# Experts' tokens placed in DRAM buckets in four groups, and the first expert steps put among the last attention tiles

## The reference

```python
x = x + L0_xattn(layernorm(x), ctx)        # 16 heads of 16
x = x + L0_ffn(layernorm(x))               # experts
x = x + L1_xattn(layernorm(x), ctx, mask)  # one head of 256
x = x + L1_ffn(layernorm(x))               # quantised linear

# L0_ffn: flat is the normalised x
probs = softmax(flat @ gate_W)             # 8 experts, the best 2 kept, weights sum to 1
out = 0.5 * gelu(flat @ shared_W + shared_b)
for e in range(8):
    out += combine[:, e] * (gelu(flat @ W1[e] + b1[e]) @ W2[e] + b2[e])
return layernorm(out) * gamma + beta
```

## Time and profile before

| | before |
|---|---|
| times of three runs, us | 1071.48, 1071.89, 1074.15 |
| the profiled execution's own time, us | 1070.92 |
| its span (first to last instruction), us | 1069.1 |
| TensorE busy | 945.4 us, 88% |
| VectorE busy | 560.1 us, 52% |
| ScalarE busy | 497.1 us, 46% |
| GpSimd busy | 539.3 us, 50% |
| mean granted TensorE clock | 0.962 |

### The profile page before, as it was taken

How to read it: one execution, slowest core, us unless ns; L and a number is a source line. 1 busy time by engine, 2 the same in 40 slices (tenths; PEclk the granted TensorE clock), 3 DMA queues, 4 the chain that set the end, 5 groups by cost and what they waited for, 6 DMA issues and landing times.

```text
span 1069.1 us, 21031 instructions
## 1 busy us (share of the span) xinstructions
PE 945.4 (88%) x7159; PEld 808.6 (76%) x7159; DVE 560.1 (52%) x1231; ACT 497.1 (46%) x1257; POOL 539.3 (50%) x654
## 2 busy tenths in 40 slices
PE   6999999999823699999999999999999989787776
PEld 4777777777612699999999999999999978554544
DVE  3888888888769223433223223322322313679882
ACT  3666666666642233333333333333333324666663
POOL 2333333333325455555565565555556532578883
PEclk9999999999955799999999999999999998999998
DMA  5434343433217521222221221222222244122201
GB/s 142 142 111 152 100 153 101 156 103 135 80 22 203 148 41 30 41 37 35 41 40 31 41 40 32 40 40 33 39 41 36 35 91 118 43 76 90 90 33 35
DMA packets 74709, 80.11 MB, mean 75 GB/s; under 512 B 12752, under 2 KB 69904, under 8 KB 74480
## 3 DMA queue, kind: packets, MB, share of 16 engines
q1 hardware_dynamic: 58704, 60.12, 18.6%
q0 software_dynamic: 15904, 18.66, 11.1%
HBM read 52.51 MB, written 26.25 MB: 74 GB/s over the span
## 4 chain that ended last, share of the span: by engine, by line
PE 60%; DVE 20%; issue 8%; POOL 6%; ACT 5%; DMA 2%; POOLq 0%; SPq 0%; DVEq 0%; ACTq 0%
PE b_H L1269 24%; PE b_Y L1281 23%; DVE a_max L635 5%; DVE a_probs L641 4%; PE a_T L506 2%; ACT a_probs L738 2%; PE a_S L496 2%; PE b_xT L1256 1%; PE c_g_ps L1940 1%; PE c_v_ps L1945 1%; POOL a_rstd L401 1%; PE c_f_ps L1911 1%; DVE a_xin L625 1%; ACT c_xn L1804 1%; DVE c_x L1773 1%
## 5 line engine op out<-in xcount | busy, mean ns | idle before, releaser
L1435 ACT ACTIVATE b_hiddenT<-b_H,b_b 128x128 f32<-128x128 f32 x568 | 162.4, 368 | 331.9 <-PE b_H L1269 331.9
L1269 PEld LDWEIGHTS b_H<-b_rowsT,b_w 128*128 128x128 f32 x2272 | 266.6, 193 | 6.0 <-ACT b_rowsT L1444 2.4
L1269 PE MATMUL b_H<-b_rowsT,b_w 128*128 128x128 f32 x2272 | 267.3, 276 | 1.8 <-ACT b_rowsT L1444 1.8
L1281 PE MATMUL b_Y<-w_sb,b_hiddenT 128*128 x1136 | 256.8, 379 | 0.0
L1227 POOL DMA_INDIRECT ffn_rows<-b_y,scatter_idx x71 | 154.0, 2169 | 193.7 <-DVE b_y L1360 185.2
L1281 PEld LDWEIGHTS b_Y<-w_sb,b_hiddenT 128*128 128x128 f32 x1136 | 210.5, 190 | 25.7
L1356 DVE TENSOR_TENSOR b_y<-b_Y,b_bc 128x256 f32<-128x256 f32 x71 | 30.2, 425 | 324.1 <-PE b_Y L1281 324.1
L1349 DVE COPY b_w<-w_sb 128x2048 f32 x71 | 87.1, 1227 | 37.5 <-issue 26.0
L635 DVE TENSOR_REDUCE a_max<-a_S 128x8 f32<-128x960 f32 x64 | 73.6, 1149 | 26.9 <-PE a_S L496 25.1
L1213 POOL DMA_INDIRECT b_rows<-xn_rows,gather_idx x71 | 73.5, 1035 | 21.5 <-issue 19.7
L744 ACT COPY a_probsT<-a_T 120x512 f32<-120x512 f32 x128 | 69.1, 594 | 28.1 <-PE a_T L506 28.1
(11 more groups left out here) (219 smaller groups left out, 1367.2 us busy)
## 6 DMA issues: line engine op xcount, KB each, us to landing
w_sb<-in_L_ffn_W SPq DMA_DIRECT2D x32, 512.0 KB, 4.5
a_xin<-in_x SPq DMA_DIRECT2D x16, 256.0 KB, 3.0
a_xres<-in_x SPq DMA_DIRECT2D x32, 128.0 KB, 2.0
xn_rows<-a_xn SPq DMA_DIRECT2D x32, 128.0 KB, 2.3
x_rows<-a_x SPq DMA_DIRECT2D x32, 128.0 KB, 2.0
ffn_rows<-shared SPq DMA_DIRECT2D x2, 2048.0 KB, 18.6
c_x<-x_rows SPq DMA_DIRECT2D x16, 256.0 KB, 2.7
c_acc<-ffn_rows SPq DMA_DIRECT2D x16, 256.0 KB, 2.7
```

The costliest lines, as they stand in the source:

```text
L1269: j = pe.matmul(H_ps[i][:, c * P:(c + 1) * P], w1c[i][:, k * HID + c * P:k * HID + (c + 1) * P], xT[:, k * P:(k + 1) * P], start=(k == 0), ...
L1281: j = pe.matmul(y_ps[i][:, 0:D], hT[i][:, c * P:(c + 1) * P], w2_sb[:, bass.ds(e * (HB * D) + c * D, D)], start=(c == 0), stop=(c == HB - 1))
L1435: j = act.activation(hT[i][:, c * P:(c + 1) * P], H_ps[i][:, c * P:(c + 1) * P], ACT.Gelu, bias=b1c[i][:, c:c + 1])
```

## The change

The routing phase is taken apart. `choose`, `count`, `places` and `put` work on four groups of eight tiles: groups 0 to 2 within the attention steps, group 3 within the expert steps. A choice isn't given a place in a list of all slots; instead `put`, an indirect DMA of GpSimd with 128 entries of 8 bytes (row number and weight), writes it to its expert's bucket in DRAM (`bucket_d`), 64 of them, 36 in the attention. Groups 0 and 1 suffice to fill 24 slot tiles (`EARLY_TILES`), `table` makes the first row and the expert of each in two parts. A slot tile's 128 entries are then fetched by SP, whose DMA takes the row from a register (`slots`, in parts of 8, 16 and 47 tiles). The buckets are filled beforehand with entries that lead to spare rows.

The steps of experts 0 and 1 begin among the products of the last attention tiles. The shared rows go to DRAM tile by tile (`shared_d`), and their gelu is taken in eight chunks of 512 KB in expert steps 1 to 4, through two buffers; only behind the last stored chunk do the scatters begin, eight results being kept. The weights of slots are no longer gathered: they come with the slots. In the last stage the mask's bounds are made there, one context is projected a cycle, and ScalarE waits for `tie` only where it uses it. `constants` is 19 GpSimd operations at t = 1, `fill_buckets` four DMAs of SP at t = 4; steps 8 to 14 prepare the last stage's weights.

The diff, cut to its core:

```diff
 SLOT_TILES = 2 * TILES + E - 1
-ROWS_Y = 2 * TOK
+EARLY_TILES = 24
+GROUPS = 4
...
+    def choose(dve, g, part):
+        lg = logits[:, g * GT * E:(g + 1) * GT * E].rearrange("p (t e) -> p t e", e=E)
+        weight = pay[:, g * GT:(g + 1) * GT]
+        if part == 0:
+            if g == 0:
+                dve.wait_ge(s_c, CONSTANTS)
...
+            done(dve, dve.reciprocal(sm[:], sm[:]))
+            done(dve, dve.tensor_tensor(pb[:], pb[:], over_e(sm[:]), ALU.mult))
+        elif part in (2, 4):
+            k = part // 2 - 1
...
+    def exps(act, g):
+        act.wait_ge(s_shift, g + 1)
+        act.activation(pb[:], pb[:], ACT.Exp).then_inc(s_exp, 1)
...
+    def count(pe, g, at):
...
+        pe.wait_ge(s_sel, g + 1)
+        flat = sel[:].rearrange("p t e -> p (t e)")
+        pe.matmul(at, before_b[:], flat, start=True, stop=False, skip_group_check=True)
+        pe.matmul(at, ones_b[:], base_b[g][:].rearrange("p t e -> p (t e)"), start=False, stop=False,
+                  skip_group_check=True)
+        for n in range(1, GT + 1):
+            i = pe.matmul(at[:, n * E:RANKS], ones_b[:], flat[:, 0:RANKS - n * E], start=False,
+                          stop=(n == GT), skip_group_check=True)
...
+    def keep_count(dve, g, at):
+        dve.wait_ge(s_rank, g + 1)
+        dve.tensor_copy(rank[:].rearrange("p t e -> p (t e)"), at).then_inc(s_rk, 1)
+    def places(dve, g):
+        dve.wait_ge(s_rk, g + 1)
+        for k in range(2):
+            done(dve, dve.tensor_tensor(tmp[:], rank[:, 0:GT], oh[k][:], ALU.mult))
+            done(dve, dve.tensor_reduce(posk[:, :, k], tmp[:], AX.X, ALU.add))
+        dve.tensor_copy(place[:, g * GT:(g + 1) * GT, :], posk[:]).then_inc(s_place, 1)
+    def put(pool, t, k):
+        g = t // GT
+        pool.wait_ge(s_place, g + 1)
+        pool.wait_ge(s_w, 2 * g + 2)
+        pool.wait_ge(s_fill, 64)
+        pool.indirect_dma_start(bucket_d, IndirectOffsetOnAxis(place[:, t, k:k + 1], 0),
+                                pay[:, t, k, :], None).then_inc(s_put[g], 16)
...
+    def table(dve, g, part):
...
+        def steps_of(t):
+            g = (t - GT - 2) // GT
+            return g, t - GT - 2 - g * GT
+        def counted(t):
+            g, step = steps_of(t)
+            return 0 <= g < GROUPS - 1 and step == 3
+        def put_in(t, k):
+            g, step = steps_of(t - 4)
+            return g * GT + step, k
...
+                if tile(t - 3):
+                    store_shared(t - 3)
+                if t == 4:
+                    routing.fill_buckets(sp)
+                if t == 5:
+                    sp.dma_start(b2_bc[:], b2.rearrange("e d -> (e d)").partition_broadcast(P)
+                                 ).then_inc(s_b12, 16)
+                    sp.dma_start(b1_rows[:], b1.rearrange("e (c p) -> (e c) p", p=P)
+                                 ).then_inc(s_b12, 16)
...
+            starts["slots"](sp, 0)
+            store_shared(TILES - 3)
             for t in (TILES - 2, TILES - 1):
                 store_xn2(t)
                 store_x2(t)
-            for u in range(2):
-                sp.wait_ge(s_x2st[u], 16 * B)
-                sp.wait_ge(s_xn2st[u], 16 * B)
+                store_shared(t)
...
+                if t >= GT + 6:
+                    routing.put(pool, *put_in(t, 0))
                 if tile(t - 1):
                     residual(t - 1)
+                    if t >= GT + 6:
+                        routing.put(pool, *put_in(t, 1))
                     inverse_std2(t - 1)
                 if u == 1 and batch(b + 2):
                     inverse_std1(b + 2)
+                if t == 1:
+                    routing.constants(pool)
+            starts["gather"](pool, 0)
             add_beta(TILES - 2)
+            starts["gather"](pool, 1)
             residual(TILES - 1)
             inverse_std2(TILES - 1)
             add_beta(TILES - 1)
+            starts["gather"](pool, 2)
...
+                if counted(t):
+                    routing.count(pe, steps_of(t)[0], counts)
...
             turn_back(t)
+            starts["rows"](pe, 0)
+            starts["first"](pe, 0, 0)
             pe.wait_ge(s_att, t + 1)
             turn_xn2(t - 1)
+            starts["first"](pe, 0, 1)
             shared_gate(t - 1)
+            starts["rows"](pe, 1)
+            starts["first"](pe, 1, 0)
             pe.wait_ge(s_sg, t)
             turn_xn2(t)
+            starts["first"](pe, 1, 1)
             shared_gate(t)
...
+                if counted(t + 2):
+                    routing.keep_count(dve, steps_of(t + 2)[0], counts)
...
+                g, step = steps_of(t)
+                if 0 <= g < GROUPS - 1:
+                    if step == 0:
+                        dve.wait_ge(s_sg, (g + 1) * GT)
+                    if step < 3:
+                        for part in range(3 * step, min(3 * step + 3, 8)):
+                            routing.choose(dve, g, part)
+                    if step == 3:
+                        routing.places(dve, g)
+                    if g == 1 and step >= 4:
+                        routing.table(dve, 0, step - 4)
+            starts["weights"](dve, 0)
...
             keep_shared(t - 1)
             normalise2(t)
+            starts["weights"](dve, 1)
             keep_shared(t)
...
+                g, step = steps_of(t)
+                if 0 <= g < GROUPS - 1 and step == 0:
+                    routing.exps(act, g)
             t = TILES - 1
             keep_probs(t, 2)
             keep_probs(t, 3)
             keep_oT(t)
+            starts["keep"](act, 0)
             keep_xn2T(t - 1)
+            starts["gelu"](act, 0, 0)
+            starts["keep"](act, 1)
+            starts["gelu"](act, 0, 1)
             keep_xn2T(t)
...
+        CHOOSE_AT, COUNT_AT, PUT_AT, CONST_AT = 1, 4, 6, 8
...
+        def slots(sp, part):
+            for g in (range(2) if part == 0 else range(2, GROUPS) if part == 2 else ()):
+                sp.wait_ge(routing.s_put[g], 16 * 2 * routing.GT)
+            sp.wait_ge(routing.s_tab, 2 if part == 2 else 1)
+            for n in range(*PARTS[part]):
+                row = sp.value_load(tile_row[0:1, n:n + 1], min_val=0, max_val=E * TOK)
+                sp.dma_start(iw[:, n, :], bucket_d[bass.ds(row, P), :]).then_inc(s_iw[part], 16)
+        def slots_there(eng, n):
+            for part, (a, b) in enumerate(PARTS):
+                if a <= n < b:
+                    eng.wait_ge(s_iw[part], 16 * (b - a))
...
+            def load_chunk(c):
+                ge(sp, s_cst[c % 2], 16 * (c // 2))
+                sp.dma_start(chunk[c % 2].rearrange("p (t d) -> p t d", d=D),
+                             shared_d[c * CHUNK // D * P:(c + 1) * CHUNK // D * P, :]
+                             .rearrange("(t p) d -> p t d", p=P)).then_inc(s_ch[c % 2], 16)
+            def store_chunk(c):
+                sp.wait_ge(s_cg, c + 1)
+                sp.dma_start(acc_d[c * CHUNK // D * P:(c + 1) * CHUNK // D * P, :]
+                             .rearrange("(t p) d -> p t d", p=P),
+                             chunk[c % 2].rearrange("p (t d) -> p t d", d=D)
+                             ).then_inc(s_cst[c % 2], 16)
+            load_chunk(0)
+            load_chunk(1)
+            slots(sp, 1)
+            for c in range(CHUNKS):
+                store_chunk(c)
+                if c + 2 < CHUNKS:
+                    load_chunk(c + 2)
+            for i in range(2):
+                sp.wait_ge(s_cst[i], 8 * CHUNKS)
...
                          ).then_inc(second["s_fw"], 16)
+            slots(sp, 2)
...
+            slots_there(pool, n)
+            ge(pool, s_xT_p, n - AHEAD + 1)
...
+            def scatter(n):
                 ge(pool, s_added, 16 * n)
+                if n == 0:
+                    for s in s_cst:
+                        pool.wait_ge(s, 8 * CHUNKS)
...
+            def scatters_at(n):
+                if n < FIRST_ADD:
+                    return ()
+                behind = 2 * (n - FIRST_ADD)
+                return (behind, behind + 1) if behind + 1 < n else (n - 1,)
+            def puts_at(n):
+                t0 = 2 * routing.GT + 2
+                done = [(t0 + j // 2, j % 2) for j in range(2 * (TILES - t0))]
+                third = 2 * (3 * routing.GT - t0)
+                if n < PUT_AT:
+                    return done[min(3 * n, third):min(3 * n + 3, third)]
+                return done[third + 4 * (n - PUT_AT):third + 4 * (n - PUT_AT) + 4]
...
+            added = 0
+            for n in range(NS):
                 if n + AHEAD - 1 < NS:
-                    gather(n + AHEAD - 1)
-                if n + 2 < NS:
-                    gather_weight(n + 2)
-                if not first:
-                    scatter(n - 1, 1 - i)
-                if last:
-                    scatter(n, i)
-            tiles(body)
+                    gather(pool, n + AHEAD - 1)
+                between = list(puts_at(n))
+                for j in scatters_at(n):
```

(40 more changed lines are left out.)

897 lines of the change are left out of this document (421 added, 476 removed).

## The result

The changed kernel takes 1078.08 us (median of 19 runs, 1072.53 to 1081.57), the kernel before 1071.89 (19 runs): ratio 1.0047, 95% interval 1.0035 to 1.0059. It is 0.5% slower; 1055 and a gain were forecast. Its profiled execution has a span of 1076.3 against 1069.1.

A forecast was written before the change was run, and what follows sets the result against it. TensorE and VectorE were taken to bound the attention, TensorE the expert steps, with 70 us between to win from. 1070.92 - 30.4 + 24 - 10.4 = 1054, median 1055 us, range 1032 to 1076.

The forecast's parts named there:

- Slots: SP's fetches by register address: 1.1 us each, bounds 0.6 and 2.6.
- rival D: A slot on SP takes 2.4; the 24 ahead of TensorE cost 31 us: 1086 us; chance 0.15.
- Boundary: Between attention and expert steps: first second product (T0) at 336.5 against 366.9, a gain of 30.4 us.
- Attention, 17: Attention grows by 17 us: VectorE's routing and table 15.5, constants and loads 1.5, GpSimd's writes hidden.
- Step 2: VectorE routing in even attention tiles: 6 operations, 1.3 us, free because they fit VectorE's idle time of 1.32.
- step 0: VectorE routing in even attention tiles: 2.1 us including ScalarE's exponent, less 1.3 idle, so 0.8 per group.
- The constants: GpSimd's 19 constants, with SP's four fills and the bias loads, cost the attention 1.5 us, between 0 and 6.
- Expert steps, 24: Expert steps lose 24 us: stall 20 from the chunks (14 before product 5), 4 from GpSimd's late gathers.
- Last stage, 10.4: Last stage gains 10.4 us: 4.2 from the later `tie` wait, 2.0 from one projection, 4.5 from the cycles, less rounding.
- The 4.5 for spreading the contexts: Last stage: one projection beside each of nine VectorE-bound cycles, about 0.5 us each, gains 4.5.
- B: Expert steps: the chunks don't hold ScalarE, slots overlap at 0.6 each, transfers from 3 us: 1033 us; chance 0.25.
- C: Attention: routing disturbs it, a `put` of 2.47 exceeds GpSimd's idle time, 12.6 us in 18 tiles: 1068; chance 0.12.

The follow-up runs named there:

- e3: Changed kernel with the mask loaded in quarters, three behind the first expert sums' loads, their bounds made in cycles 0, 3 and 7: ratio 1.0068 to the kernel before.
- e4: Changed kernel with eight contexts projected ahead of the last stage's cycles and two in each of the first four, as before: ratio 1.0113 to the kernel before.
- e5: The changed kernel again, unaltered, on another chip: ratio 1.0100 to the kernel before, median 1087 us, runs from 1076.6 to 1091.1.
- e8: Changed kernel without the shared rows' way through the chunks (zeros stored, nothing loaded, no gelu of them): ratio 0.9875 to the kernel before.
- e1: Changed kernel with SyncE's 16 slots of the second part fetched three at a time between chunk store and next load: ratio 0.9995 to the kernel before.
- e6: e1 without the 28 bucket writes that GpSimd does in the expert steps: ratio 0.9860 to the kernel before, its two runs 1054.1 and 1065.1 us.
- e12: e1 with the 28 late bucket writes replaced by 28 gathers of the same 128 rows of 8 bytes into SBUF: ratio 0.9971 to the kernel before.
- e9: e1 with late bucket writes spread two, then three a step, GpSimd waiting ahead of them for the previous step's second product: ratio 0.9970 to the kernel before.
- e11: e9 plus one chunk a step, respaced scatters, quartered mask, contexts as in e4, and VectorE's routing mainly in even attention tiles: ratio 0.9791 to the kernel before.
- e17: The changed kernel a third time, unaltered, on one chip with e18: ratio 1.0057 to the kernel before.
- e14: e9 plus one chunk a step, respaced scatters, quartered mask and contexts as in e4, but without GpSimd's waits: ratio 0.9739 to the kernel before, 1043.3 us.
- e18: The kernel of e14 once more, beside the changed kernel on another chip: ratio 0.9730 to the kernel before, 1043.0 us.

## Why the prediction was wrong

- **Slots.** 1.08 to 1.10 us each in the profile after, as forecast, and rival D's 2.4 in none. But in e3, e4, e5 and e8 the sixteen ahead of the chunks took 1.84 to 1.92 each, beyond the 1.8 from which D was to decide; e5 is the same kernel, at 1087. Even there they didn't act as in D: TensorE, itself waiting 12.6 us for instructions, then waited 11.2 ahead of product 5, less than the 15.6.
- **Boundary.** From the turn of the last tile to T0 22.6, forecast 319.5 - 296.3 = 23.2; the 3.9 of new idle time are 4.9. Right in size.
- **Attention, 17, measured 22.8.** The step that failed is "Step 2 (even) 6 operations, 1.3: nothing, it fits the idle time", and step 0's 0.8. The idle time is there only while TensorE holds its clock; e5's tile of 8.53 against 10.60 shows it. The tiles at a lower clock make 4.5 of the 22.8; the sum had the clock at full there. Step 0 was priced 0.8 too low even at full clock. The constants were over-priced by 1 to 1.5.
- **Expert steps, 24, measured 35.4** from T0 to the last result (509.9 before, 545.4 after). The chunks stall TensorE as forecast: the wait ahead of product 5 is 15.6 (14), a cycle of the ring 5.6 (5.2), the last chunk has landed at T0 + 66 (62), and the three waits are 19.9 in sum (20). The step that failed is the sum "Together 24", which adds waits only. Left out: TensorE comes out of each stall at its lower clock, 6.44 for 3.73, 5.47 for 3.73, 4.6 us in all. Left out too: GpSimd waits for `rows_stored` until 345.0, so TensorE waits 1.9 for gather 3. GpSimd's backlog was 4 in the sum; a step takes it 11 us (10), and TensorE lost 5.6 in three waits for gathers and 1.7 of clock. That makes 33.7; the other 1.7 lie in no wait that I found.
- **Last stage, 10.4, measured 3.1** from the last result to the end (192.4, 189.3). The tie's wait and the projection gave 4.0 of their 6.2: ScalarE copied at once, but then waited 3.68 for GpSimd's `c_x_nb`, whose sums were late. That wait goes back to "the mask is asked for some 12 us before that wait starts", a sentence that looked at the mask as a wait only. It is also traffic: 2 to 3 us (e3). The 4.5 for spreading the contexts wasn't met: it gave -1.9 to -1.5 in the three profiles of the changed kernel, and +3.5 and +4.8 in e1 and e6. In e1 the first cycles ran at a higher clock; here too the sum had it at full. A cycle with one projection takes 9.7, without 8.9, and the old ones with two 11.2 on average, so nine times 0.8 against four times 2.3 leaves 2.
- **Rivals.** B (chunks don't hold ScalarE) is refuted by the 15.34, C by the writes of at most 1.28. The other side came not by my rival D, one mechanism of 31 us, but by two under-sized terms and an over-sized gain, 5.8, 11.4 and 7.3, less 0.6 at the boundary: 23.9, and 1054 + 23.9 is the profiled execution (1078).

What stays open: TensorE's waits for its own instructions. What the profiles show: in e1 to e8 except e6, and in e12, they are 7 to 13 us in the steps, mostly in the first 30 us. DMA queues also carry instructions, and the first such transfer more than 10 us behind T0 comes 28 to 31 us behind it in these eight profiles and 17 to 22 in all others (359.7 after; 371.2 and 370.3 in e4 and e5). Which is cause and which effect isn't shown. Without GpSimd's late writes (e6) and with a pause ahead of them (e9) the waits are gone, each in one profile (e11, also paced, has 3.5), reads do as well as writes (e12), chunks don't matter (e8). But on the last two chips no kernel had them in the steps, among them the changed kernel (e17) and the unpaced combination (e14, e18), and there the times spread over 2 to 10 us where e5's spread over 14. GpSimd's unbroken run of transfers is therefore likely, but not shown, to be a condition: it was not enough in the profile after, in e14, e17 and e18. What the other one is, chip or execution, these runs don't tell.

## What to carry to other kernels

Price a queue's order, not only its instructions: sixteen fetches of 1.08 us ahead of the first store made TensorE wait 15.57 us, and in e18 the same fetches, put where SyncE waits for a store to land, left TensorE busy 102 of 105 us. Work that fits an engine's idle time is free only if no other engine has to pause for it: look at the granted clock behind each new pause, give each new stall a second price for the next stretch at the lower clock, and don't take one profile for the rule, as the clock fell in different tiles of the same kernel. Draining a backlog of scatters at twice the steady rate moved the stall to the gathers; with four in three steps, and the bucket writes spread, it vanished (e18).

## What the runs showed of the hardware

A 128-row gather or bucket write takes GpSimd 0.95 to 1.10 us, now and then up to 2.0, the accumulating scatter 1.55 to 2.6, and in a run without a pause one was issued every 1.28. During such runs TensorE got its matmuls late on three of the five chips of e1 to e18, in e1 one or two at a time and 0.7 to 2.1 us apart, and SyncE was slow with it: sixteen slots took 29.4 to 30.8 us in e3, e4, e5 and e8, against 17.24. The same attention tile took 8.53 us at a granted clock of 1.00 and 10.60 at 0.68. A mask load of 2 MB held SyncE's next three issues for 8.35 us (1.78 behind a quarter of it, e3), and a scatter beside it landed after 8.6 us, where the median is 4.5.
